# Weighted sums with features on partitions, and maxima turned by VectorE instead of TensorE

## The reference

```python
# B, L, H = 16, 512, 256; 16 heads of 16
q = heads(x @ Wq)
out_short = softmax(q @ k_s.T / 4 - |i - j| * (1 - decay)) @ v_s
out_long  = softmax(q @ k_l.T / 4) @ v_l
out = (sigmoid(mix) * out_short + (1 - sigmoid(mix)) * out_long) @ Wo
x1 = layernorm(x + out)                 # (16, 512, 256)
# then 16 steps of a gated recurrence over x1, an output projection, tanh, residual, layernorm
```

## Time and profile before

| what | value |
|---|---|
| median of 3 runs | 2155.01 us (2152.42 to 2155.71) |
| profiled execution, time | 2155.48 us |
| its span, first to last instruction | 2153.6 us |
| mean granted TensorE clock | 0.989 |

### The profile page before, as it was taken

How to read it: one execution, slowest core, us unless ns; L and a number is a source line. 1 busy time by engine, 2 the same in 40 slices (tenths; PEclk the granted TensorE clock), 3 DMA queues, 4 the chain that set the end, 5 groups by cost and what they waited for, 6 DMA issues and landing times.

```text
span 2153.6 us, 40927 instructions
## 1 busy us (share of the span) xinstructions
PE 2084.7 (97%) x16544; PEld 1129.1 (52%) x16544; DVE 1624.0 (75%) x2083; ACT 1462.5 (68%) x1750; POOL 131.9 (6%) x186
## 2 busy tenths in 40 slices
PE   6999999999999999999999999999999988999997
PEld 3444444444444444444444444444444437888887
DVE  6788888888888888888888888888888854333346
...
DMA packets 91263, 134.32 MB, mean 62 GB/s; under 512 B 21300, under 2 KB 43572, under 8 KB 91076
## 3 DMA queue, kind: packets, MB, share of 16 engines
...
## 4 chain that ended last, share of the span: by engine, by line
PE 90%; ACT 4%; DVE 3%; issue 2%; ACTq 0%; DMA 0%; POOL 0%; SPq 0%; DVEq 0%; POOLq 0%
PE pv_ps L722 21%; PE pair_ps L658 17%; PE work L626 15%; PE banks L1140 13%; PE pair_ps L684 13%; PE work L788 3%; PE pair_ps L634 3%; ACT probs L391 3%; PE banks L1180 2%; DVE maxes L581 1%; PE banks L1133 1%; PE banks L1187 1%; PE work L792 1%; DVE res L563 1%; PE work L775 0%
## 5 line engine op out<-in xcount | busy, mean ns | idle before, releaser
L581 DVE TENSOR_REDUCE maxes<-pair_ps 128x2 f32<-128x1024 f32 x1024 | 1228.2, 1222 | 239.2 <-PE pair_ps L634 154.1
L391 ACT ACTIVATE probs<-pair_ps,small 128x1024 f32<-128x1024 f32 x512 | 563.1, 1113 | 226.3 <-PE pair_ps L634 224.7
L391 ACT ACTIVATE probs<-pair_ps 128x1024 f32<-128x1024 f32 x512 | 516.7, 1024 | 159.7 <-PE pair_ps L658 154.6
L722 PE MATMUL pv_ps<-probs,vals 128*32 128x512 f32 x4096 | 547.3, 606 | 0.3 <-ACT probs L391 0.3
L658 PE MATMUL pair_ps<-q_op,k_op 56*128 56x512 f32 (+1 forms) x2048 | 480.0, 478 | 13.8 <-ACT probs L391 10.5
L684 PE MATMUL pair_ps<-k_op,q_op 55*128 55x512 f32 x2048 | 433.9, 431 | 7.2 <-ACT probs L391 4.6
L658 PEld LDWEIGHTS pair_ps<-q_op,k_op 56*128 56x128 f32 (+1 forms) x2048 | 191.8, 184 | 445.2 <-DVE maxes L581 205.6
L684 PEld LDWEIGHTS pair_ps<-k_op,q_op 55*128 55x128 f32 x2048 | 195.9, 186 | 152.1 <-issue 107.3
L634 PE MATMUL pair_ps<-eye_b,tri_b 64*128 64x64 bf16 x4096 | 163.1, 194 | 0.0
L634 PEld LDWEIGHTS pair_ps<-eye_b,tri_b 64*128 64x128 bf16 x4096 | 94.0, 95 | 114.3 <-issue 95.7
L722 PEld LDWEIGHTS pv_ps<-probs,vals 128*32 128x32 f32 x4096 | 80.7, 108 | 98.1 <-issue 87.8
...
## 6 DMA issues: line engine op xcount, KB each, us to landing
k_op<-kq_h SPq DMA_DIRECT2D x508, 64.0 KB, 2.2
q_op<-kq_h SPq DMA_DIRECT2D x256, 64.0 KB, 2.2
k_op<-kq_l SPq DMA_DIRECT2D x254, 64.0 KB, 2.2
x_step<-in_xT ACTq DMA_DIRECT2D x16, 512.0 KB, 3.8
q_op<-kq_l SPq DMA_DIRECT2D x128, 64.0 KB, 2.2
x_res<-in_x ACTq DMA_DIRECT2D x16, 512.0 KB, 3.9
x_dram<-res ACTq DMA_DIRECT2D x16, 512.0 KB, 2.9
x_back<-x_dram SPq DMA_DIRECT2D x16, 512.0 KB, 4.3
```

The lines of the kernel that those rows point to most:

```text
L391: act.activation(probs[:, s % 2, 2 * hp:2 * hp + 2, :], pairs_ps[pair_of(b, s, "b", hp)][:, :, :], ACT.Exp, scale=LAM if s // 4 % 2 else 1 ...
L581: dve.reduce_max(maxes[:, u % 2, :, hp, s % 4], pairs_ps[pair_of(b, s, "a", hp)][:, :, :], mybir.AxisListType.X).then_inc(a_reduced, 1)
L722: last = pe.matmul(pv_ps[32 * h:32 * h + 32, :], vals[:, c, g // 2, att, at:at + 32], probs[:, s % 2, h, :], start=(c == 0), stop=(c == TC ...
```

## The change

The weighted sums are no longer turned. SP moves the rows of `pv_sb` by four DMAs a unit into `o_att`, now with features on partitions, and gathers the four rows of denominators by a fifth into `dens`, 16 to a partition (`move_sums`). DVE inverts half a batch's denominators at once, in place (`invert`, slots 2 and 18). SP stores them to DRAM in the next slot (`store_inverses`) and in the slot behind it loads them back with each row repeated over 16 partitions (`load_inverses`). POOL multiplies both attentions by the inverses and adds them; the sum lies as the output projection wants it. ACT makes its high part (`high_part`, slots 9 and 29) and POOL the low part. The maxima are turned by DVE in 32x32 blocks, with `maxes` padded to 32 columns for each of its two places, and SP copies them in four pieces of 32 queries; the sign moves into the constant rows of the k operand. PE has no "turn" and no "ot" tasks any more; "v" and "wo" tasks have other slots. On POOL, x's low part comes first in a batch. Two memsets move from DVE to POOL.

```diff
-TASKS = {0: ("ot", 0, -1), 2: ("v", (4,), 0), 3: ("v", (5,), 0), 4: ("v", (6,), 0), 6: ("ot", 1, -1), 7: ("v", (7,), 0),
-         8: ("wo", (0,), -1), 12: ("wo", (1,), -1), 16: ("wo", (2, 3), -1), 20: ("v", (0, 1), 1), 24: ("v", (2,), 1), 28: ("v", (3,), 1)}
+TASKS = {0: ("v", (3,), 0), 2: ("v", (4,), 0), 3: ("v", (5,), 0), 4: ("v", (6,), 0), 6: ("v", (7,), 0),
+         12: ("wo", (0,), -1), 16: ("wo", (1,), -1), 20: ("wo", (2, 3), -1), 24: ("v", (0, 1), 1), 28: ("v", (2,), 1)}
...
-TASKS |= {4 * m + 1: ("turn", m, 0) for m in range(UNITS)}
+INVERT, STORE_INVERSES, LOAD_INVERSES, HIGH_PART = ({at: (1, -1), at + 16 + later: (0, 0)} for at, later in ((2, 0), (3, 0), (4, 0), (9, 4)))
...
-        o_att = [sb(f"o_att{a}", [P, TC, NH, HD]) for a in range(2)]
-        o_sum = sb("o_sum", [P, TC, H])
+        o_att, inverses = sb("o_att", [P, 2, KC, L]), sb("inverses", [P, 2, L])
+        o_sum = sb("o_sum", [P, KC, L])
+        dens = sb("dens", [P, KC, 2, 2, HD])
+        inv_dram = nc.dram_tensor("inv_dram", [KC, 2, 2, GH * L], F32, kind="Internal").ap()
...
-        maxes = sb("maxes", [P, 2, 2, GH // 2, TC])
-        shift_rows = sb("shift_rows", [GH * TC, 2, P], F32R)
+        maxes = sb("maxes", [P, 2, 2 * GH * TC], F32R)
+        maxima = [maxes[:, a, 0:GH * TC].rearrange("p (h m c) -> p h m c", h=2, m=GH // 2) for a in range(2)]
...
+            def move_maxima(b, u):
+                if exists(b):
+                    wait(sp, done["shift"], b, UNITS, u + 1)
+                    row = MAX_ROW + u % 2
+                    to = q_op[u // 2][row:row + HALF + 1:HALF, :, :].rearrange("r h (t n) -> r (h t) n", n=P)
+                    for at in range(0, P, 32):
+                        copy_words(to[:, :, at:at + 32], shift_rows[at:at + GH * TC, u % 2, :]).then_inc(shift_loaded[u % 2], 16)
+            def move_sums(b, u):
+                if exists(b):
+                    g, att = u // 2, u % 2
+                    wait(sp, pv_copied, b, UNITS, u + 1)
+                    wait(sp, inv_stored, b, 16 * 2, 16 * (u // 4 - 1))
+                    sp.dma_start(dens[:, g // 2, att, g % 2, :], pv_sb[HD:P:32, att, :]).then_inc(sums_moved[att], 16)
+                    wait(sp, osum_done, b, 2, u // 4 - 1)
+                    for h in range(GH):
+                        to = HALF * (g % 2) + HD * h
+                        sp.dma_start(o_att[to:to + HD, att, g // 2, :], pv_sb[32 * h:32 * h + HD, att, :]).then_inc(sums_moved[att], 16)
+            def store_inverses(b, k):
+                if exists(b):
+                    wait(sp, inverted, b, 2, k + 1)
+                    for a in range(2):
+                        wait(sp, inv_loaded[a], b, 16 * 2, 16 * (k - 1))
+                    sp.dma_start(inv_dram[k].rearrange("a g (p e) -> p (a g) e", p=P), dens[:, k, :, :, :].rearrange("p a g e -> p (a g) e")).then_inc(inv_stored, 16)
+            def load_inverses(b, k):
+                if exists(b):
+                    wait(sp, inv_stored, b, 16 * 2, 16 * (k + 1))
+                    for a in range(2):
+                        wait(sp, scaled, b, 4, 2 * k)
+                        rows = inv_dram[k, a].rearrange("g (h n) -> (g h) n", n=L)
+                        sp.dma_start(inverses[:, a, :], rows.unsqueeze(1).to_broadcast([2 * GH, HD, L])).then_inc(inv_loaded[a], 16)
...
-                    if s in TASKS and TASKS[s][0] == "turn":
-                        _, maxima = turned(b, TASKS[s][1])
-                        if maxima:
-                            bb, u = maxima
-                            wait(sp, done["shift"], bb, UNITS, u + 1)
-                            row = MAX_ROW + u % 2
-                            copy_words(q_op[u // 2][row:row + HALF + 1:HALF, :, :].rearrange("r h (t n) -> r (h t) n", n=P),
-                                       shift_rows[:, u % 2, :]).then_inc(shift_loaded[u % 2], 16)
+                    if s % 4 == 1:
+                        move_maxima(*unit_of(b, s // 4 + 1))
+                        move_sums(*sums_before(b, s // 4))
+                    for slots, move in ((STORE_INVERSES, store_inverses), (LOAD_INVERSES, load_inverses)):
+                        if s in slots:
+                            k, off = slots[s]
+                            move(b + off, k)
...
+            move_sums(B - 1, UNITS - 1)
+            store_inverses(B - 1, 1)
+            load_inverses(B - 1, 1)
...
+            pool.memset(vals[:, :, :, :, :], 1.0).then_inc(ones_set, 1)
+            pool.memset(maxes[:, :, :].bitcast(F32), 0.0).then_inc(ones_set, 1)
...
-                def add_attentions(bb, n):
-                    wait(pool, done["pvt"], bb, UNITS, UNITS // 2 * (n + 1))
-                    o = [a[:, :, NH // 2 * n:NH // 2 * (n + 1), :].rearrange("p t h d -> p t (h d)") for a in o_att]
-                    pool.tensor_tensor(o_sum[:, :, P * n:P * n + P], o[0], o[1], ALU.add).then_inc(osum_done, 1)
+                def add_attentions(bb, k):
+                    for a in range(2):
+                        wait(pool, inv_loaded[a], bb, 16 * 2, 16 * (k + 1))
+                        pool.tensor_tensor(o_att[:, a, k, :], o_att[:, a, k, :], inverses[:, a, :], ALU.mult).then_inc(scaled, 1)
+                    wait(pool, scaled, bb, 4, 2 * k + 2)
+                    wait(pool, done["ot"], bb, 2, k - 1)
+                    pool.tensor_tensor(o_sum[:, k, :], o_att[:, 0, k, :], o_att[:, 1, k, :], ALU.add).then_inc(osum_done, 1)
+                def low_part(bb, k):
+                    wait(pool, ot_hi, bb, 2, k + 1)
+                    wait(pool, full["wo"], bb, 4, 0)
+                    pool.tensor_tensor(ot_l[:, k, :], o_sum[:, k, :], ot_h[:, k, :].bitcast(F32), ALU.subtract).then_inc(done["ot"], 1)
                 bb = b - 1
-                if exists(bb):
-                    add_attentions(bb, 1)
                 if b >= 0 and exists(b + 1):
                     wait(pool, xt_hi, b + 1, 1, 1)
                     pool.tensor_tensor(xt_l[(b + 1) % 2][:, :, :], xt_in, xt_h[(b + 1) % 2][:, :, :].bitcast(F32),
                                        ALU.subtract).then_inc(xt_lo, 1)
-                if exists(b):
-                    add_attentions(b, 0)
+                if exists(bb):
+                    add_attentions(bb, 1)
+                    low_part(bb, 1)
...
+                if exists(b):
+                    add_attentions(b, 0)
+                    low_part(b, 0)
...
+                wait(act, sums_moved[u % 2], b, 80 * UNITS // 2, 80 * (u // 2))
                 act.activation(pv_sb[:, u % 2, :], pv_ps[:, :], ACT.Copy).then_inc(pv_copied, 1)
+            def high_part(b, k):
+                if exists(b):
+                    wait(act, osum_done, b, 2, k + 1)
+                    wait(act, full["wo"], b, 4, 0)
+                    act.activation(ot_h[:, k, :], o_sum[:, k, :], ACT.Copy).then_inc(ot_hi, 1)
...
+                    if s in HIGH_PART:
+                        k, off = HIGH_PART[s]
+                        high_part(b + off, k)
...
-            def turn(b, m):
-                sums, maxima = turned(b, m)
-                wait(dve, full["turn"], b, UNITS, m + 2)
-                if maxima:
-                    bb, u = maxima
-                    wait(dve, shift_loaded[u % 2], bb, 16 * UNITS // 2, 16 * (u // 2))
-                    dve.tensor_scalar(shift_rows[:, u % 2, :].rearrange("p (g e) -> p g e", e=GAP), turned_maxima, -1.0, None,
-                                      ALU.mult).then_inc(done["shift"], 1)
-                if sums:
-                    bb, u = sums
-                    g, att = u // 2, u % 2
-                    o = work[:, :].rearrange("p (t h e) -> p t h e", t=TC, h=GH)
-                    dve.reciprocal(rden[:, att, :, :], o[:, :, :, HD]).then_inc(rden_done, 1)
-                    wait(dve, rden_done, bb, UNITS, u + 1)
-                    if u < 2:
-                        wait(dve, osum_done, bb, 2, 0)
-                    dve.tensor_tensor(o_att[att][:, :, GH * g:GH * g + GH, :], o[:, :, :, 0:HD],
-                                      rden[:, att, :, :].unsqueeze(3).to_broadcast([P, TC, GH, HD]),
-                                      ALU.mult).then_inc(done["pvt"], 1)
+            def turn(b, u):
+                if exists(b):
+                    wait(dve, a_reduced, b, 8 * UNITS, 8 * u + 8)
+                    wait(dve, shift_loaded[u % 2], b, 64 * UNITS // 2, 64 * (u // 2))
+                    dve.transpose(shift_rows[:, u % 2, :].bitcast(F32), maxes[:, u % 2, :].bitcast(F32)).then_inc(done["shift"], 1)
+            def invert(b, k):
+                if exists(b):
+                    for a in range(2):
+                        wait(dve, sums_moved[a], b, 80 * UNITS // 2, 80 * (2 * k + 2))
+                    dve.reciprocal(dens[:, k, :, :, :], dens[:, k, :, :, :]).then_inc(inverted, 1)
...
                     if s % TC == 0:
+                        turn(*unit_of(b, s // 4 + 1))
                         reduce(1)
...
```

(33 more changed lines are left out.)

64 lines of the change are left out of this document (24 added, 40 removed).

## The result

The changed kernel takes 2128.54 us (median of four, 2128.37 to 2132.73) where the kernel before takes 2155.36 beside it: the ratio is 0.9876, with a 95% interval of 0.9865 to 0.9888. That is 27 us less where 63 were predicted. It is faster as forecast and lies inside the stated range of 2046 to 2165, but outside the 2065 to 2120 of the forecast's own case.

The account below looks back on a forecast made before the run. TensorE's own instruction stream was taken as the bound: 6.8 us a batch off, 2.4 us of new waits on, so 4.4 x 15.5 = 68.2 us off and 5.0 on, from 2155.5 to 2092.3 us; range 2046 to 2165.

Parts of the forecast that it names:

- the forecast's own case: Whole kernel: 2065 to 2120 us, with the new waits varied between bounds; chance 0.47.
- What leaves PE: Turns of sums and maxima, 5.6 us, and transpositions of summed attention, 1.2 us: 6.8 us a batch off TensorE.
- The new waits: Waits the change adds in each batch, four terms summing to 2.4 us.
- (c): Slots 8 and 9, no task left on PE: DVE's two reductions and transposition take longer; 0.4 us a batch.
- (d): The three bank pairs shared by ACT and DVE come round sooner; 0.3 us a batch more waiting on PE.
- buffers and late shift rows eat it: Rival: two 2 us waits for shift rows, 1.5 us for banks; batch 106 to 107 us, 2120 to 2150; chance 0.17.
- (a): Slots 2 and 18: DVE's inversion waits for sums SP moves one slot before; 0.65 us twice, 1.3 us a batch.
- (b): SP's queue: store and load of inverses stand ahead of shift rows for slots 8 and 24; 0.2 us twice.
- SyncE as the bound: Rival: new DMA issues over 0.81 us each make SP's queue set the time; 2263 us at 0.90; chance 0.15.
- DVE's new instructions: Eight 128x64 block transpositions at 0.25 us and two reciprocals at 0.3 us: 2.6 us a batch added on DVE.
- The number of batches: Steady stretch from about 67 us to 1749 us: 15.5 batches' worth, multiplying the 4.4 us saved in each.
- The end of attention: Last unit's inverses have no cover: output matmuls 2.4 us later, 2.6 us for a slower clock; +5.0 us.

Follow-up runs that it names:

- e15: The kernel before with ScalarE's exponentials over the first 256 of each 512 queries alone; 2128.41 us.
- e12: The changed kernel with ScalarE's exponentials over the first 256 of each 512 queries alone; 2076.5 us.
- e1: The changed kernel with five transpositions of the identity put back on TensorE where the old turn stood, in each slot 4m+1; 2160.24 us.
- e10: The changed kernel with inversion, store and load of the inverses and high part one slot later; 2126.8 us.
- e2: The changed kernel without the four DMAs of each unit that move the weighted sums into o_att; the denominators' gather stays; 2119.2 us.
- e9: The kernel before with the change's five DMAs a unit added in SyncE's queue, into tiles that nobody reads; 2162.8 us.

## Why the prediction was wrong

**The bound before** was read rightly: TensorE's stream. e15 puts it within 1.8 us of the 108.2 us batch.

**What leaves PE**: 6.8 us a batch were forecast; e12 and e15 together give 6.4.

**The new waits** are the step that failed, in its terms (c) and (d). For slots 8 and 9 the prediction took 0.4 us, and for the ring everywhere else 0.3 us, "with the present slack". Together 0.7; measured are about 4: the batch fell by 2.4 where 6.4 left, and the moves (0.10) and the inverses' place (0.14) are only 0.24 of the rest, hardly clear of the noise.

In (c) the prediction asked only whether DVE keeps up in slots 8 and 9. It left out that slot 7 loses its task too, and that there PE waits for an exponential which has only just been able to start. Slots 7 and 8 cost 1.4 us.

In (d) it built on the slack of an engine over a batch (ACT 27 us without work, DVE 17), which says nothing of the ring: three pairs of banks let TensorE run ahead by three fills, less than a slot. In slots 4m+1 ACT's copy of 0.6 us and three exponentials stand in a row, and DVE's two reductions take 2.4 us. The turn covered the waits for these: with a filler in its place (e1) those for DVE and for the copy all but vanish. In the earlier trace rows only 0.6 us of wait showed there, since a turn of 0.70 us stood on top of the rest. Of the 4.0 us, 1.7 go with ACT's exponentials alone (e12 less e15).

The rival "buffers and late shift rows eat it" (2120 to 2150, given 0.17) was the right one, through the buffers alone: it had 1.5 us for them and 4 for shift rows, so its batch of 106 to 107 us is near 105.8 by a sum whose parts are wrong. The range held the result because it takes in this rival. By the bounds of the forecast's own terms all at their upper end, 6.5 us of waits, that case would have reached 2156 and not 2120.

**(a) and (b)**: DVE waits 1.0 us a batch before its inversion; the prediction had 2.6 and charged 1.3. It costs some 0.14, because half a wait was charged where nearly all of it was slack. For shift rows PE's matmuls don't wait once in the 13 batches, and its weight loads seven times, 6.0 us in all; in e10 neither waits, and its batch is the same but for 0.14 us. The wait of 2.9 us stands in the last batch. So (a) and (b), charged with 1.7 us together, came out near nothing, which hid part of the error in (c) and (d).

**SyncE as the bound** didn't come: issues of 0.37 to 0.67 us, as taken. That the gather would land later, which the prediction took from the Trainium skill's rule ("DMA: Bandwidth & Descriptors", section "Why a DMA increments its semaphore by 16 and not by 1"), isn't borne out. In the changed kernel the wait for sums ended on the moves of `o_att`. In e2, where only the gather is left, DVE's inversion started 2.84 us after the gather's issue began (371.34 to 374.18 us) without a wait, so the gather had landed within 2.25 us of the end of its issue of 0.59. How many engines it ran on no run shows.

**DVE's new instructions**: the transposition is 128x32, not 128x64 as the prediction said, and took 0.202 us for the 0.25 assumed; the reciprocal of 64 elements took 0.548 for 0.3.

**The number of batches**, 15.5, was too high. Up to ACT's last exponential the changed kernel is 30.0 us ahead, which is 12.5 times 2.4. By place: 0.8 us are gained ahead of the second low part of x, 31.1 in the 13 batches between the second and the last, and 2.0 are lost behind it. The last batch makes no scores for the maxima of a next one and has the recurrence's weights on ACT; in the kernel before, PE's waits for exponentials are 10.6 us from 1540 us on, where they are 2.3 in all 13 batches. So less of what leaves PE can come back there, and e2 and e9 put 5 to 6 us of the moves' cost there. With 13 batches the forecast of 4.4 would have been 57 us, not 68.

**The end of attention**: +5.0 forecast, +3.0 measured (382.0 for 379.0). The output matmuls start 2.1 us later behind ACT's last exponential, where 2.4 were worked out, and from their start to the next matmuls it takes 1.7 us longer (5.47 for 3.74), at a granted clock of 0.64 from 1764.4 to 1770.0 us, where 2.6 were charged for the clock. 0.8 us comes back behind them. The chain of the changed kernel, to be set beside the earlier trace rows:

```profile
1745.77 0.61 ACT pv_sb L477
...
1748.84 2.44 DMA o_att<-pv_sb
...
1751.96 2.26 DMA inv_dram<-dens
1754.24 3.88 DMA inverses<-inv_dram
...
1764.44 1.65 PE work L676 x6
```

From the copy to the output matmuls it takes 18.7 us, where 19.1 were worked out. The sum goes by these: 2155.5 − 30.0 + 3.0 = 2128.5.
